# A two-layer cross-attention kernel: projections and energies of a pair moved one iteration up, beside the scores of the pair two ahead of it

## The chip, the cores and the metric

The kernel runs on one core of a Trainium2 chip. The metric is the device time of one execution in microseconds (us); less is better.

## The reference

The input is a batch of 32 items. All arithmetic is float32. Layer 0 mixes x (128 x 512 an item) with a context y of the same shape, layer 1 is an attention with 32 query heads over 8 key heads and a layer norm:

```python
def layer0(x, y, w_qk, w_v, b_v, w_t, b_t):          # x, y: (32, 128, 512)
    x_q = einsum('oc,bcn->bno', w_qk, y)
    x_k = einsum('oc,bcn->bon', w_qk, x)
    x_v = einsum('oc,bcn->bon', w_v, x) + b_v
    attention = softmax(einsum('bnc,bcm->bnm', x_q, x_k), axis=-1)
    attention = attention / (1e-07 + attention.sum(axis=1, keepdims=True))
    x_r = einsum('bcn,bnm->bcm', x_v, attention)
    return x + relu(einsum('oc,bcn->bon', w_t, x - x_r) + b_t)

def layer1(h, enc, mask, ...):                       # 32 heads of 16, 8 key heads, groups of 4
    q, k, v = h @ Wq + bq, enc @ Wk + bk, enc @ Wv + bv
    attn = softmax(q k^T / 4 + mask)                 # by head
    x = (attn v) @ Wo + bo + h
    return layernorm(x) * gamma + beta

return layer1(layer0(x, ctx, ...), ctx, mask, ...)
```

## The kernel before

The batch is worked in 16 pairs of items, j = 0 and 1. Each float32 product is made of reduced-precision parts: an operand is split in a high part, rounded by a copy into type fp32r, and a low part, the difference; a product is then high x high, high x low and low x high, three matmuls. So `xh`, `xl` are the parts of x, `yh`, `yl` of the context, `zh`, `zl` of z = (w_qk^T w_qk) x, and so on.

A pair passes through four stages, and an iteration i of the program works on several pairs at once:

- stage 0: `z_project(i)` computes z of pair i + 1.
- stage 1, pair i: `energy` (8 a pair, en00 to en13, three matmuls of 512 columns each), whose negated row maxima VectorE takes (`energy_max`) and whose exponentials ScalarE writes to `att` (`exp_energy`); `tva_project` (8 a pair: values, transposed x and more, in one), copied by ScalarE (`tva_raw`) and biased and scaled on GpSimd (`add_bias`, `scale_values`); `attend`, which sums values by attention; `layer0_out` on VectorE, which ends layer 0 and writes `x2`; `ctx_transpose` and `kv_project` for the keys and values of layer 1; `spread_k` on GpSimd.
- stage 2, pair q = i - 1: `q_project` (4 groups g), its parts `q_high` on ScalarE and `q_low` on VectorE; `max_scores`, four matmul blocks that compute all scores once for their maxima alone, and 16 `score_max` on VectorE; `max_split` makes `mrow` of them, `max_spread` turns it on TensorE, `max_rows` copies it to `mrep`; SyncE copies `qh`, `ql` into `qstack` with 12 DMAs (`stack_q`, which waits for `ql_done` of the last group) and `mrep` with one more (`stack_maxima`). Only then can `scores` run (16 blocks), ScalarE takes their exponentials (`exp_scores`), `values` sums them, `keep_sums` copies the sums to `sides`, two DMAs gather the denominators (`gather_denominators`), VectorE inverts them (`inverse_denominators`, `weigh_out`), and `at_high`, `at_low` split the result for `out_project` (wo0 in the same iteration, wo1 in the next).
- stage 3, pair i - 2: wo1, the residual add and statistics, variance and inverse root on GpSimd in small steps, `normalise`, `scale_shift`, `store`.

Each engine runs its own instructions in the written order of its function `iteration` (also `first_iteration` and `last_iteration`); semaphores connect them. Iterations 3 to 14 are a hardware loop; the rest are written out. PSUM has eight banks, handed out in a ring in the order of `WIDE_USES` (line 80): a use takes the next bank and, by `wait_slot`, waits until the use eight before it in the list has been read (`RELEASE`, line 288; for a maxima block that is its `score_max`, for a z the `z_low`). A line of this table:

```python
    ("mx01", 2), ("mx02", 2), ("mx03", 2), ("q1", 2), ("q2", 2), ("mx10", 2), ("mx11", 2), ("mx12", 2),
```

The tiles `xh`, `yh` are made on GpSimd as a product with ones (`split_x`, `split_y`, line 514), followed there by the low parts. On SyncE, the loads of the next x and y stand at `next_x`, `next_y`; `next_y(i)` waits for `ctx_transpose(i, 1)`, since the transposes read the same tile. A second copy of TensorE's program with mask matmuls (L853, L877) is taken only if the mask isn't zero; it is zero here.

## Time and profile before

| | |
|---|---|
| median of 3 runs | 855.9 us (855.87 to 859.55) |
| the profiled execution, its own time | 855.26 us |
| its span in the profile | 853.4 us |
| TensorE matmuls, busy | 763.5 us (89%) |
| VectorE | 612.0 us (72%) |
| GpSimd | 567.1 us (66%) |
| ScalarE | 481.4 us (56%) |
| mean granted TensorE clock | 0.965 |
| DMA moved | 84.88 MB |

PE is TensorE, DVE is VectorE, ACT is ScalarE, POOL is GpSimd, SP is SyncE (SPq its DMA queue). The span runs from the first to the last recorded instruction. A row in order of time gives start and length in us, and in brackets how long the engine stood idle ahead of it and which instruction released it. Matmuls overlap, so the distance of their starts and not their length is what one costs.

### The profile page before, as it was taken

Reading aid. Unit: us, or ns where it says so; the run is one execution under the profiler, and the core shown is the slowest. Engines: PE = TensorE matmul, PEld = TensorE weight load, DVE = VectorE, ACT = ScalarE, POOL = GpSimd, SP = SyncE. Lnnn points to the kernel's source line nnn. Section 1 sums busy time; section 2 is a strip of 40 time slices with the busy share of each in tenths; the row PEclk is TensorE's granted clock in tenths of the full one; section 3 lists DMA queues with packets and bytes.
Section 4 is the critical chain, followed back from the end, with each engine's and each line's share of the span. In section 5 each row is a group of like instructions: output and inputs, shape, how many; then the busy total and the mean of one; then the engine's idle time right before and its main releaser. Section 6 shows DMA issues by size and latency. Waiting matters only on the chain.

```text
span 853.4 us, 17328 instructions
## 1 busy us (share of the span) xinstructions
PE 763.5 (89%) x5015; PEld 603.7 (71%) x5015; DVE 612.0 (72%) x1016; ACT 481.4 (56%) x1067; POOL 567.1 (66%) x770
## 2 busy tenths in 40 slices
PE   5878989989898999989899999989899998988672
PEld 4766877858687786868687786868778686866531
DVE  4675876948687695958679595868869585976733
ACT  4637475564746557384756747474665738474250
POOL 4945677585766859486785948577694958664513
PEclk9889999999999999999999999999999999999776
DMA  8124242323434242343424233343413234332410
GB/s 312 67 65 114 84 112 77 99 78 111 108 97 127 74 108 74 104 120 109 103 86 118 81 93 102 111 101 98 132 68 104 77 111 114 93 77 89 95 62 25
DMA packets 55756, 84.88 MB, mean 99 GB/s; under 512 B 9520, under 2 KB 29616, under 8 KB 55600
## 3 DMA queue, kind: packets, MB, share of 16 engines
q1 hardware_dynamic: 55008, 84.25, 34.0%
q10 hardware_dynamic: 720, 0.27, 0.2%
q8 instruction: 15, 0.25, 0.1%
q14 instruction: 13, 0.11, 0.0%
HBM read 24.72 MB, written 8.39 MB: 39 GB/s over the span
## 4 chain that ended last, share of the span: by engine, by line
PE 65%; SPq 13%; DMA 7%; DVE 6%; issue 4%; POOL 3%; ACT 2%; DVEq 0%; POOLq 0%; ACTq 0%
PE banks L784 13%; SPq L374 13%; PE banks L875 8%; PE banks L888 7%; DMA qstack<-mrep 5%; PE banks L900 4%; PE banks L902 4%; PE banks L901 4%; PE banks L822 3%; DVE maxima L1522 3%; PE banks L824 3%; PE banks L823 3%; PE banks L803 2%; PE banks L846 2%; DVE ql L1515 2%
## 5 line engine op out<-in xcount | busy, mean ns | idle before, releaser
L1522 DVE TENSOR_REDUCE maxima<-banks 128x4 f32<-128x512 f32 x256 | 161.2, 688 | 8.2 <-PE banks L846 8.2
L1183 ACT ACTIVATE prob<-banks 128x512 f32<-128x512 f32 x256 | 133.4, 634 | 11.4 <-PE banks L875 11.4
L1547 DVE RECIPROCAL dens<-dens 128x512 f32<-128x512 f32 x32 | 107.3, 3353 | 39.5 <-DMA dens<-sides 39.5
L784 PE MATMUL banks<-ta,att 128*128 128x130 f32 x1024 | 119.8, 275 | 2.7 <-POOL ta L556 2.7
L784 PEld LDWEIGHTS banks<-ta,att 128*128 128x128 f32 x1024 | 118.1, 190 | 4.8 <-POOL ta L556 3.4
L1117 ACT ACTIVATE att<-banks,negmax 128x512 f32<-128x512 f32 x128 | 87.7, 688 | 51.7 <-DVE negmax L1472 51.7
L1472 DVE TENSOR_REDUCE negmax<-banks 128x1 f32<-128x512 f32 x128 | 86.6, 688 | 31.9 <-PE banks L771 30.6
L875 PE MATMUL banks<-qstack,kstack 128*128 128x512 f32 x256 | 77.8, 429 | 27.8 <-DMA qstack<-mrep 26.6
L621 POOL TENSOR_TENSOR atl<-at,ath 128x512 fp32r<-128x512 f32 x32 | 43.7, 1364 | 72.6 <-ACT ath L1195 72.1
L875 PEld LDWEIGHTS banks<-qstack,kstack 128*128 128x128 f32 x256 | 48.7, 200 | 57.9 <-issue 34.0
L549 POOL TENSOR_TENSOR ta<-ta,cb_s 128x516 f32<-128x516 f32 x64 | 76.8, 1210 | 17.1 <-ACT ta L1125 17.1
L1466 DVE TENSOR_TENSOR zl<-banks,zh 128x512 fp32r<-128x512 f32 x32 | 21.9, 685 | 77.1 <-ACT zh L1110 77.1
L822 PE MATMUL banks<-x2h,wq_h 128*128 128x256 f32 x256 | 75.3, 294 | 0.0
L824 PE MATMUL banks<-x2h,wq_l 128*128 128x256 f32 x256 | 72.2, 282 | 0.0
L823 PE MATMUL banks<-x2l,wq_h 128*128 128x256 f32 x256 | 72.1, 281 | 0.0
L1189 ACT ACTIVATE sides<-banks 128x512 f32<-128x512 f32 x64 | 39.4, 617 | 56.2 <-PE banks L888 53.3
L1195 ACT ACTIVATE ath<-at 128x512 fp32r<-128x512 f32 x32 | 20.1, 628 | 90.0 <-PE banks L902 83.4
L888 PE MATMUL banks<-prob,v 128*32 128x512 f32 x512 | 66.9, 616 | 1.2 <-ACT prob L1183 1.2
L1168 ACT ACTIVATE qh<-banks,bq_s 128x256 fp32r<-128x256 f32 x64 | 30.4, 475 | 64.5 <-PE banks L824 64.5
L1125 ACT ACTIVATE ta<-banks 128x386 f32<-128x386 f32 x128 | 60.4, 490 | 10.6 <-PE banks L759 10.6
L900 PE MATMUL banks<-wo_h,ath 128*128 128x512 f32 x128 | 54.9, 429 | 9.1 <-POOL atl L621 9.1
L561 POOL TENSOR_TENSOR late<-late,bo_b 128x512 f32<-128x512 f32 x32 | 41.1, 1286 | 30.9 <-ACT late L1174 30.9
(145 smaller groups left out, 2011.2 us busy)
## 6 DMA issues: line engine op xcount, KB each, us to landing
qstack<-qh SPq DMA_DIRECT2D x128, 128.0 KB, 2.3
xs<-in_x SPq DMA_DIRECT2D x16, 512.0 KB, 3.6
ys<-in_ctx SPq DMA_DIRECT2D x16, 512.0 KB, 3.5
kstack<-kph SPq DMA_DIRECT2D x128, 64.0 KB, 2.0
qstack<-ql SPq DMA_DIRECT2D x64, 128.0 KB, 2.3
dens<-sides SPq DMA_DIRECT2D x64, 128.0 KB, 2.0
out_x<-late SPq DMA_DIRECT2D x32, 256.0 KB, 2.1
kstack<-kpl SPq DMA_DIRECT2D x64, 64.0 KB, 2.0
```

What stands on the lines that cost most here:

```text
L374: sp.dma_start(qstack[32 * part:32 * part + 32, p].bitcast(F32), src[32 * p:32 * p + 32].bitcast(F32)).then_inc(qstack_in[p], 16)
L784: last = mm(o, att[:, j, n, bass.ts(m, P)], ta[:, j, n, 0:BW], start=n == 0, stop=n == KC - 1)
L822: mm(o, wq_h[:, k, g], x2h[:, k], start=k == 0, stop=False)
L823: mm(o, wq_h[:, k, g], x2l[:, k], start=False, stop=False)
L824: last = mm(o, wq_l[:, k, g], x2h[:, k], start=False, stop=k == KC - 1)
L875: last = mm(o, kstack[:, j, 2 * p + odd], qstack[:, p, j], start=True, stop=not masked)
L888: last = mm(banks[32 * p:32 * p + 32, slot(plan, name)], v2[:, j, 2 * p + odd], prob[:, 2 * p + odd], start=True, stop=True, tile_position ...
L900: mm(o, ath[:, g], wo_h[:, g], start=g == 0, stop=False)
L1117: nc.scalar.activation(att[:, j, n], banks[:, slot(plan, f"en{j}{n}")], exp_f, bias=negmax[:, j, n:n + 1], accum_out=rowsum[:, j, n:n + 1] ...
L1183: nc.scalar.activation(prob[:, 2 * p + odd], banks[:, slot(plan, f"st{j}{kv}")], exp_f).then_inc(sem["prob_done"], 1)
L1522: nc.vector.tensor_reduce(maxima[:, 0, :, p, :, g].rearrange("x o j -> x j o"), banks[:, slot(plan, f"mx{g}{p}")].rearrange("x (j o s) -> ...
L1547: nc.vector.reciprocal(dens[:], dens[:]).then_inc(sem["dinv_done"], 1)
```

## The change

The numbers of the two projections' stage change from 1 to 0: `tva_project`, `energy`, and what follows them (`tva_raw`, `exp_energy`, `energy_max`, `row_inverse`, `add_bias`, `scale_values`) now run in iteration i for pair i + 1, while `attend`, `layer0_out`, `ctx_transpose`, `kv_project` stay at pair i. A first iteration numbered -1 runs them for pair 0, and iteration 15 has none. `xh` and `yh` are now written by ScalarE (`x_high`, `y_high`), `at_low` is moved from GpSimd to VectorE, both `x2_low` stand in their own pair's iteration, and every engine's order and the ring's order are rewritten. The core of the diff (the other lines are of the same kind: calls in another order):

```diff
 WIDE_USES = (
-    ("en00", 1), ("en01", 1), ("en02", 1), ("wo1", 3), ("q0", 2), ("tva00", 1), ("en03", 1), ("mx00", 2),
...
+    ("q0", 2), ("q1", 2), ("q2", 2), ("mx00", 2), ("mx01", 2), ("mx02", 2), ("mx03", 2), ("wo1", 3),
+    ("mx10", 2), ("mx11", 2), ("mx12", 2), ("mx13", 2), ("q3", 2), ("et0", 1), ("et1", 1), ("mx20", 2),
+    ("mx21", 2), ("mx22", 2), ("mx23", 2), ("mx30", 2), ("mx31", 2), ("mx32", 2), ("mx33", 2), ("z0", 0),
+    ("b00", 1), ("b01", 1), ("r0", 2), ("r1", 2), ("tva00", 0), ("m", 2), ("k", 1), ("tva01", 0), ("en00", 0),
...
-                RELEASE[f"tva{j}{k}"] = ("ta_raw", 4 * j + k, 1)
-                RELEASE[f"en{j}{k}"] = ("exp_done", 4 * j + k, 1)
+                RELEASE[f"tva{j}{k}"] = ("ta_raw", 4 * j + k, 0)
+                RELEASE[f"en{j}{k}"] = ("exp_done", 4 * j + k, 0)
...
             def split_x(i, j):
-                if j == 0:
-                    pool.wait_ge(x_in, i * 16 + 16)
+                wait(pool, "xh_done", i, j)
                 wait(pool, "tva_ps", i - 1, 4 * j + 3)
-                nc.gpsimd.tensor_tensor(xh[:, j], xs[:, j], one_col, ALU.mult).then_inc(sem["xh_done"], 1)
-                wait(pool, "xh_done", i, j)
                 nc.gpsimd.tensor_tensor(xl[:, j], xs[:, j], xh[:, j].bitcast(F32), ALU.subtract
...
             def x2_low(i, j):
                 wait(pool, "x2h_done", i, j)
+                wait(pool, "k_ps", i, 0)
                 wait(pool, "v_ps", i, 0)
...
-            def energy(i, plan, j, n):
+            def energy(pair, plan, i, j, n):
                 name = f"en{j}{n}"
                 if n == 0:
-                    wait(pe, "zl_done", i, j)
-                    wait(pe, "y_split", i, j)
-                wait_slot(pe, plan, name, i)
+                    wait(pe, "zl_done", pair, j)
+                    wait(pe, "y_split", pair, j)
+                wait_slot(pe, plan, name, i, have=("zl_done", 1, j))
...
+            def x_high(i, j):
+                if j == 0:
+                    act.wait_ge(x_in, i * 16 + 16)
+                wait(act, "tva_ps", i - 1, 4 * j + 3)
+                nc.scalar.activation(xh[:, j], xs[:, j], copy_f).then_inc(sem["xh_done"], 1)
...
+            def at_low(q, j):
+                wait(dve, "ath_done", q, j)
+                wait(dve, "wo_ps", q, j - 1)
+                tt(atl[:], at[:].rearrange("p (g l) -> p g l", g=G), ath[:].bitcast(F32), ALU.subtract
+                   ).then_inc(sem["atl_done"], 1)
...
             def first_iteration(i, load_next, s1, s2, s3, setup=False):
                 if load_next:
                     next_x(i)
                 if s1:
                     next_mask(i)
-                if setup:
-                    load_late_weights()
                 if load_next:
                     next_y(i)
                 if setup:
+                    load_late_weights()
                     gather_flags()
```

In `last_iteration` (16) wo1 stands behind the maxima, both `residual_transpose` at the end behind wo0, and `values` for both odd and even heads of half 0 directly behind its eight scores.

**TensorE between the last maxima blocks and the scores, iteration 2.** L846 (now L820) is a maxima block, L757 to L759 (L731 to L733) a `tva_project`, L793 a context transpose, L832 (L806) both residual transposes, L861 (L835) `max_spread`, L769 to L771 an energy, L718 to L720 a z, L758 both `attend` of j = 0. Before:

```order
L793 MATMUL banks<-cst,ys 128x128 x4
L757 MATMUL banks<-cw_h,xh 128x386
L758 MATMUL banks<-cw_h,xl 128x386
L759 MATMUL banks<-cw_l,xh 128x258
L793 MATMUL banks<-cst,ys 128x128 x4
L832 MATMUL banks<-cst,x 128x128 x8
L861 MATMUL banks<-ident_r,mrow 128x128
L769 MATMUL banks<-zh,yh 128x512
L770 MATMUL banks<-zl,yh 128x512
L771 MATMUL banks<-zh,yl 128x512
```

and now, from the last maxima block on:

```order
L820 MATMUL banks<-kph,qh 128x256 x8
L827 MATMUL banks<-mk,cst 128x256 x8
L718 MATMUL banks<-xh,gram_h 128x512
L719 MATMUL banks<-xl,gram_h 128x512
L720 MATMUL banks<-xh,gram_l 128x512
L758 MATMUL banks<-ta,att 128x130 x16
L806 MATMUL banks<-cst,x 128x128 x8
L731 MATMUL banks<-cw_h,xh 128x386
L732 MATMUL banks<-cw_h,xl 128x386
L733 MATMUL banks<-cw_l,xh 128x258
L835 MATMUL banks<-ident_r,mrow 128x128
```

Ahead of `max_spread` now stand z and `attend` of j = 0; behind it, ahead of the scores, came three energies and now come the k projection, two `tva_project` and one energy.

**VectorE from the start of iteration 2 to the last maxima.** L1515 (L1519) is `q_low`, L1522 (L1526) `score_max`, L1472 `energy_max`, L1558 (L1568) the residual add, L1562 `at_low`, L1507 a context low part. Before:

```order
L1472 TENSOR_REDUCE negmax<-banks 128x1 x2
L1558 TENSOR_TENSOR late<-banks,late 128x512
L1472 TENSOR_REDUCE negmax<-banks 128x1
L1563 BN_STATS bns<-late 128x6
L1515 SCALAR_TENSOR_TENSOR ql<-banks,bq_s,qh 128x2x128
L1472 TENSOR_REDUCE negmax<-banks 128x1
L1522 TENSOR_REDUCE maxima<-banks 128x2x2 x2
L1568 TENSOR_SCALAR yi<-nv 128x2
L1522 TENSOR_REDUCE maxima<-banks 128x2x2
L1515 SCALAR_TENSOR_TENSOR ql<-banks,bq_s,qh 128x2x128
L1522 TENSOR_REDUCE maxima<-banks 128x2x2 x3
L1515 SCALAR_TENSOR_TENSOR ql<-banks,bq_s,qh 128x2x128
```

and now:

```order
L1562 TENSOR_TENSOR atl<-at,ath 128x512
L1519 SCALAR_TENSOR_TENSOR ql<-banks,bq_s,qh 128x2x128 x3
L1526 TENSOR_REDUCE maxima<-banks 128x2x2 x4
L1568 TENSOR_TENSOR late<-banks,late 128x512
L1526 TENSOR_REDUCE maxima<-banks 128x2x2 x2
L1573 BN_STATS bns<-late 128x6
L1526 TENSOR_REDUCE maxima<-banks 128x2x2
L1519 SCALAR_TENSOR_TENSOR ql<-banks,bq_s,qh 128x2x128
L1526 TENSOR_REDUCE maxima<-banks 128x2x2
L1507 TENSOR_TENSOR x2l<-banks,x2h 128x4x128 x2
L1526 TENSOR_REDUCE maxima<-banks 128x2x2 x3
```

Three `q_low` stand ahead of the first maximum, and the energy maxima between them are gone; the two context low parts stand in front of the third block, and `at_low` at the iteration's end.

**SyncE at the start of the program.** Before, from the second load of x on:

```order
L351 DMA xs<-in_x 128x2x512
L357 DMA mk<-in_mask 128x2x128
L405 DMA late<-in_Wq 128x4x512
L407 DMA bo_b<-in_bo 128x512
L407 DMA gamma_b<-in_gamma 128x512
L407 DMA beta_b<-in_beta 128x512
L409 DMA prob<-in_Wo 128x4x512
L354 DMA ys<-in_ctx 128x2x512
L414 DMA flag_row<-flag_col 1x128x2
```

and now:

```order
L351 DMA xs<-in_x 128x2x512
L357 DMA mk<-in_mask 128x2x128
L354 DMA ys<-in_ctx 128x2x512
L405 DMA late<-in_Wq 128x4x512
L407 DMA bo_b<-in_bo 128x512
L407 DMA gamma_b<-in_gamma 128x512
L407 DMA beta_b<-in_beta 128x512
L409 DMA prob<-in_Wo 128x4x512
L414 DMA flag_row<-flag_col 1x128x2
```

The load of the next y (`ys`), which waits for the context transposes of pair 0, stood behind the late weights and stands ahead of them.

## Rows read from the trace of the kernel before

**Rows 1.** Busy time by window: start:end, length, per engine, granted clock, DMA share, GB/s.
```profile
73.40:225.90 152.50, 143.46 (x939) 113.55 (x939) 111.15 (x186) 88.40 (x197) 102.53 (x143) 0.97 0.33 94
225.90:714.90 489.00, 464.29 (x3130) 369.38 (x3130) 371.92 (x620) 293.55 (x661) 352.45 (x481) 1.00 0.35 100
763.30:811.00 47.70, 36.77 (x254) 28.71 (x254) 29.23 (x51) 19.07 (x40) 23.44 (x39) 0.89 0.30 82
811.00:853.40 42.40, 20.41 (x72) 10.71 (x72) 13.90 (x12) 12.19 (x23) 11.53 (x28) 0.70 0.12 44
```

**Rows 2.** TensorE in order of time, one iteration: start, length, line, operation [idle before].
```profile
401.15 0.28 PE L822 MATMUL banks<-x2h,wq_h 128*128 128x256 f32 x1
...
402.58 0.34 PE L757 MATMUL banks<-cw_h,xh 128*128 128x386 f32 x1
...
411.82 0.44 PE L757 MATMUL banks<-cw_h,xh 128*128 128x386 f32 x1 [0.34 <-DVE maxima L1522]
...
417.52 0.32 PE L861 MATMUL banks<-ident_r,mrow 128*128 128x128 f32 x1 [0.32 <-DVE mrow L1537]
...
421.68 2.33 PE L875 MATMUL banks<-qstack,kstack 128*128 128x512 f32 x9 [1.52 <-DMA qstack<-mrep]
...
447.14 0.50 PE L900 MATMUL banks<-wo_h,ath 128*128 128x512 f32 x1
...
450.05 0.28 PE L822 MATMUL banks<-x2h,wq_h 128*128 128x256 f32 x1
```

**Rows 3.** The chain of waits in the same iteration: start, length, what.
```profile
411.29 0.57 SPq L374
...
418.91 2.55 DMA qstack<-mrep
```

**Rows 4.** TensorE in order of time, the first scores of iterations 1 and 2.
```profile
73.40 3.78 PE L875 MATMUL banks<-qstack,kstack 128*128 128x512 f32 x9 [1.88 <-DMA qstack<-mrep]
...
123.58 2.90 PE L875 MATMUL banks<-qstack,kstack 128*128 128x512 f32 x9 [1.99 <-DMA qstack<-mrep]
```

**Rows 5.** VectorE in order of time, the iteration of rows 2.
```profile
403.48 0.48 DVE L1515 SCALAR_TENSOR_TENSOR ql<-banks,bq_s,qh 128x256 fp32r<-128x256 f32 x1 [0.25 <-ACT qh L1168]
...
411.08 5.47 DVE L1522 TENSOR_REDUCE maxima<-banks 128x4 f32<-128x512 f32 x9
...
417.10 0.29 DVE L1537 TENSOR_REDUCE mrow<-maxima 128x64 fp32r<-128x128 f32 x1
```

**Rows 6.** TensorE in order of time, the start of the program.
```profile
20.17 0.69 PE L757 MATMUL banks<-cw_h,xh 128*128 128x386 f32 x1 [2.90 <-ACT att L1117]
...
33.28 3.84 PE L784 MATMUL banks<-ta,att 128*128 128x130 f32 x32 [1.51 <-POOL ta L556]
...
47.30 0.77 PE L769 MATMUL banks<-zh,yh 128*128 128x512 f32 x1 [2.75 <-issue]
50.03 0.59 PE L770 MATMUL banks<-zl,yh 128*128 128x512 f32 x1 [1.96 <-issue]
```

**Rows 7.** Single lines (ns min/median/max), and one group (busy us, mean ns).
```profile
L1553 DVE TENSOR_TENSOR at<-sides,dens x32: 691/693/1017, 87.8 to 832.9; 128x512 f32<-128x512 f32 x32
...
L1163 ACT ACTIVATE x2h<-x x32: 619/630/634, 45.5 to 789.5; 128x512 fp32r<-128x512 f32 x32
...
L621 POOL TENSOR_TENSOR atl<-at,ath 128x512 fp32r<-128x512 f32 x32 | 43.7, 1364 | 72.6 <-ACT ath L1195 72.1
```

**Rows 8.** SyncE in order of time, the start.
```profile
9.73 0.47 SPq L405 DMA_DIRECT2D late<-in_Wq  x1
```

**Rows 9.** TensorE in order of time, iterations 15 and 16.
```profile
763.33 2.32 PE L875 MATMUL banks<-qstack,kstack 128*128 128x512 f32 x9 [1.71 <-DMA qstack<-mrep]
...
807.51 0.47 PE L861 MATMUL banks<-ident_r,mrow 128*128 128x128 f32 x1 [4.82 <-DVE mrow L1537]
...
811.05 4.16 PE L875 MATMUL banks<-qstack,kstack 128*128 128x512 f32 x10 [1.34 <-DMA qstack<-mrep]
...
836.45 0.50 PE L900 MATMUL banks<-wo_h,ath 128*128 128x512 f32 x1 [2.12 <-POOL atl L621]
```

670 lines of the change are left out of this document (340 added, 330 removed), and 31 rows, old and new, of tables (FIRST_WIDE_USES, LAST_WIDE_USES, WIDE_USES).

## The prediction

> **What bounds the kernel now.** I read the windows by stage first. From 225.9 to 714.9 us ten iterations take 489.0 us, 48.9 each, and TensorE is busy for 464.3 of them; VectorE, the next, for 371.9 [rows 1]. So the reader is to see a matmul-bound loop with some 2.5 us an iteration in which TensorE stands still. The second view, TensorE's timeline, says where most of it lies: 0.34 us on a maxima bank, 0.32 on `mrow`, and 1.52 on the DMA of the maxima, ahead of the scores [rows 2]. Work is then 46.4 us. The third view is the chain of waits: SyncE issues the twelve stack DMAs behind `ql_done` from 411.29, comes to the DMA of `mrep` at 418.91, 7.6 later, and that DMA takes 2.55 us until the scores may go [rows 3]. Early on the same wait was longer, 1.88 and 1.99 us, and the score matmuls behind it were slow: 9 in 3.78 and 2.90 us, where 2.33 is usual [rows 4, 2]. The granted clock of that stretch is 0.97 against 1.00 later [rows 1]. Last, the two ends: iteration 16 holds only one pair's attention, and from 763.3 to 853.4 TensorE is busy for 57 us of 90 [rows 1].
>
> The sum is made against this execution: span 853.4, own time 855.26, so 1.86 lie around the span; own time is 0.6 below the median of 855.9.
>
> **Inside an iteration.** I walk the new order by rows of the old one. Time 0 is the first matmul of `q_project(0)`. A projection takes 402.58 - 401.15 = 1.43, the out-projection 450.05 - 447.14 = 2.91 [rows 2]. VectorE gives `ql` 2.33 after its projection began (403.48 - 401.15), a maximum every 0.605 (5.47 over 9), and from the last of them to `mrow` done pass 0.8 [rows 5].
> - VectorE's order now has `ql` 0, 1, 2 ahead of the first maximum. `ql` 2 starts at 2 x 1.43 + 2.33 = 5.2, so the maxima start at 5.6. Behind stand 16 maxima (9.7), `ql` 3 (0.4), the residual add, the statistics and two context subtractions (0.6 each) and the guess (0.1): 18.2; `mrow` is done at 19.0.
> - TensorE reaches the third block of maxima at about 10.8 (four projections, two blocks of maxima, out-projection, context transposes). But the ring of eight banks gives it one bank per reduced maximum: `mx33` needs `etl` 1, at 13.35, and `z0`, next in the ring, needs the maximum of `mx20`, at 13.96. It starts at 14.05. TensorE had 1.1 us of work there, some 2.2 to 2.5 idle. **The wait on the maxima DMA is so replaced by a wait on banks.**
> - From 14.05: z 0.8, attend 3.6 to 3.8 [rows 6], residual transposes 0.95, one projection 0.57: `max_spread` at 20.0, not held by `mrow` (19.0). `mrep` is copied by 20.6, its DMA takes 2.55 [rows 3], the scores may go at 23.4. TensorE meanwhile has k, two projections and an energy, 3.5 us, and comes to the scores at 23.8. That wait is gone, the stack DMAs too (11.5 + 7.6 = 19.1, ahead of `mrep`).
> - The rest is 46.4 less the 21.4 done, 25.0: end at 48.8 to 49.0. I followed the banks there: `kl` is ready 0.3 before `st04` asks, score banks come free 0.5 apart, `en03` needs the values' bias at 40.6 and comes at 41.8. None costs over 0.3; I count 0.1.
> - Idle 2.45 is what it was (2.5), so +0.1 with those. The idle now ends in blocks over 1.88 us, where the early rows show the clock fall [rows 4]. A fall over score matmuls cost 1.45 and 0.57. Here it falls on z and on attend, whose 32 loads-and-matmuls took 3.84 at a mixed clock [rows 6] against 3.7: I take half of 0.7, +0.3. **Period 49.3**, bounds 47.2 (no bank wait counts) and 50.5 (each wait drops the clock at full price).
>
> **Engines beside it.** ScalarE gets four copies of 128x512 an iteration, 0.63 each [rows 7]; it is busy 29.4 us of 48.9 [rows 1] and they stand where it waited for projections, so zero; without that cover, 2.5 us an iteration. GpSimd loses 60 products and 32 `at_low`. `x_split` still comes behind the variance on GpSimd at 13.8 and just meets `z0`; were it late, it adds one for one. `at_low` goes to VectorE, two an iteration; the nearest row there with two SBUF inputs, `at`, has 0.69 on the median and 1.02 at most, I take 0.8; GpSimd took 1.36 [rows 7]. VectorE ends its iteration at 52.4, that is 3.4 into the next, and `ql` 2 is due at 5.2: 1 us to spare after `ql` 0 and 1. Zero. On SyncE, x and y are loaded ahead of `stack_q`; x lands before 9, first used at 11.6; y is issued at 10.9 and SyncE is free again before `ql_done` at 11.5.
>
> Some `at` took 1.02 where most took 0.69, so something did hold them [rows 7]. The Trainium skill, SBUF — State Buffer, section Who interferes with whom, says of the pair of ports that VectorE and GpSimd share that a VectorE operation with two SBUF inputs and a GpSimd operation lock each other out for the whole instruction. By that rule an `at_low` that meets a GpSimd operation waits for all of it, and the move costs what rival 3 works out from rows, 854 in place of 846.
>
> **Head.** Before, the scores of iteration 1 began at 73.40 [rows 4]. Now pair 0's projections and energies are in iteration -1 (no mask sums on ScalarE ahead of them) and end at about 22.5, against the 2.9 us wait of before; attends run 23.4 to 30.8, where they stood from 33.28 on [rows 6]. Pair 1's z, 8 projections and 8 energies, 11 us, come into iteration 0, paced by VectorE (two `layer0_out`, the selectors, `wq_l`, energy maxima): end at 47.5, an estimate of mine and the weakest number here. The flag's load and jump then cost the 2.75 + 1.96 of before [rows 6]. First `q_project` at 52, scores 23.8 later: 76. **+2.6**. SyncE: `load_late_weights` was issued at 9.73 [rows 8]; now `next_y(0)` is ahead of it and waits for pair 0's context transposes, at 23.4; the weights then land by 33, before `wq_l` needs them at 44. Bounds: 72 to 80.
>
> **Iteration 15 and the end.** Iteration 15 now has no projections, z or energies: 11.3 us less on TensorE. It is then bound by VectorE and the denominators: maxima chain as above, scores at 22.4, last `at_low` at 46.0. Iteration 16's maxima need 12.1 more of VectorE, `mrow` at 58.1, scores at 61.7, 39.3 after those of 15. Before it was 811.05 - 763.33 = 47.7, with 4.82 lost on `mrow` [rows 9]. **-8.4**; bounds -5 and -10. From there to the end 42.4 [rows 1]: both o-values of half 0 come earlier by about 1, and an `at_low` of 0.7 to 0.8 in place of 1.36 is in the chain twice (2.12 of wait ahead of the last out-projection [rows 9]). **-2.1**; bounds 0 and -3.
>
> **Sum.** Scores 1 to scores 15 took 763.33 - 73.40 = 689.9 [rows 9, 4]. Now 14 x 49.3 less 1.4, since iteration 15 comes to its scores earlier: 688.8, **-1.1** (the early slow scores go, the steady ones cost a little). 853.4 + 2.6 - 1.1 - 8.4 - 2.1 = 844.4; with 1.86 around it **846**. With the terms' bounds together, its own range is 838 to 854.
>
> **Rivals.**
> 1. *Slower: the bank wait drops the clock in each iteration.* Place: TensorE ahead of `z_project(0)`. Full price 1.45 [rows 4, 2] instead of 0.3: 14 x 1.15 = 16, so 862. It decides where the walked idle of 2.2 to 2.5 is real: 1.52 left the clock up [rows 2], 1.88 and 1.99 did not [rows 4]. Against: small matmuls lie in it, and attend is bound by weight loads. The Trainium skill, TensorE: Matmul & The Clock Gate, section HAM oscillation, says that a wait that comes back each tile can start the array slow each time; the early rows agree, the steady 1.52 do not. Chance 0.17.
> 2. *No wait at all.* If banks come free earlier than I walked (VectorE starts its maxima sooner), 2.1 of the idle goes: 14 x 2.1 = 29, so 817. For: VectorE is idle 11.7 us an iteration [rows 1]. Against: the ring ties TensorE to it just here. Chance 0.12.
> 3. *The order is better but VectorE is not.* Each `at_low` held by a GpSimd operation, 0.69 + 1.36 = 2.0 instead of 0.8 [rows 7]: 2.4 more an iteration, 1 of it covered; with half of them met, some 0.6 x 14 = 8, so 854. Or the late weights hold iteration 1 by 5: 851. Or it does not do what it says, the two ends' gains failing: 855. Chance 0.13.
>
> **Chances.** A measurement of this kernel can tell 0.5%, 4.3 us: faster is below 851.6, slower above 860.2. Forecast 0.58, of it 0.05 above 851.6. Faster 0.53 + 0.12, same 0.05 + 0.13, slower 0.17, rounded to 0.66, 0.18, 0.16. The range takes in the forecast's own, most of rival 3, and reaches into rivals 1 and 2, leaving 0.2 out: 830 to 860.
>
> **What will show it.** Idle ahead of the scores near zero and some 2 us ahead of `gram_h` z matmuls, put down to maxima; scores 49.3 apart; scores 1 near 76; scores 15 to 16 near 39. It is wrong if idle of over 1 us stands at the scores again, if `ql` waits for VectorE's end of the iteration before, or if the clock of the steady stretch is below 0.97.

## The result, and the profile after

The changed kernel took 865.25 us (median of 4 runs, 863.56 to 865.70), the kernel before beside it 857.02 (4 runs, 855.87 to 859.55): a ratio of 1.009, with an interval of 1.006 to 1.012. It is 0.9% **slower**, where I had forecast 846. The profiled execution took 863.56, its span is 861.8.

The first lines of the page, busy time by engine:

```profile
PE 777.9 (90%) x5015; PEld 623.9 (72%) x5015; DVE 623.3 (72%) x1048; ACT 504.4 (59%) x1128; POOL 473.8 (55%) x677
```

ScalarE and VectorE have more to do than before, GpSimd 93 us less, as the diff says. TensorE has the same 5015 matmuls and is busy 14 us longer: the same work runs slower. Windows of the profile after, columns as in [rows 1]:

```profile
229.43:730.54 501.11, 477.37 (x3131) 384.07 (x3131) 376.31 (x641) 309.17 (x701) 294.21 (x420) 0.98 0.34 98
355.10:404.04 48.94, 46.58 (x314) 37.30 (x313) 37.61 (x65) 30.84 (x71) 29.42 (x42) 1.00 0.35 100
404.04:454.62 50.58, 48.20 (x315) 38.81 (x313) 37.66 (x65) 30.96 (x71) 29.38 (x42) 0.97 0.33 97
778.53:821.23 42.70, 33.11 (x199) 24.00 (x200) 27.64 (x41) 15.27 (x33) 13.51 (x17) 0.86 0.33 92
821.23:861.80 40.57, 20.10 (x80) 11.78 (x80) 15.94 (x15) 14.67 (x27) 18.59 (x46) 0.71 0.12 46
```

The first line holds the same ten iterations as the second of [rows 1] (scores 4 to scores 14): 501.1 us instead of 489.0. The second and third are two neighbouring iterations, 7 and 8: 48.94 us at clock 1.00, and 50.58 at 0.97. By stage, with the forecast beside it:

| stretch (starts on TensorE) | before | forecast | after |
|---|---|---|---|
| start to scores 1 | 73.4 | 76 | 81.6 |
| scores 1 to 15 | 689.9 | 688.8 | 697.0 |
| scores 15 to 16 | 47.7 | 39.3 | 42.7 |
| scores 16 to the end | 42.4 | 40.3 | 40.6 |

**Inside iteration 8.** TensorE in order of time, columns as in [rows 2]; L796 is the first query projection, L820 a maxima block, L874 wo1, L718 z, L758 attend, L849 the scores:

```profile
404.04 0.28 PE L796 MATMUL banks<-x2h,wq_h 128*128 128x256 f32 x1
...
409.70 0.71 PE L820 MATMUL banks<-kph,qh 32*128 32x256 f32 x8 [1.18 <-DVE ql L1519]
410.34 0.50 PE L874 MATMUL banks<-wo_h,ath 128*128 128x512 f32 x1
...
417.57 0.38 PE L820 MATMUL banks<-kph,qh 32*128 32x256 f32 x2 [0.49 <-DVE maxima L1526]
418.17 0.38 PE L820 MATMUL banks<-kph,qh 32*128 32x256 f32 x1 [0.21 <-DVE x2l L1507]
418.76 0.50 PE L820 MATMUL banks<-kph,qh 32*128 32x256 f32 x5 [0.22 <-DVE x2l L1507]
419.54 0.50 PE L718 MATMUL banks<-xh,gram_h 128*128 128x512 f32 x1 [0.27 <-POOL xl L508]
...
420.57 5.14 PE L758 MATMUL banks<-ta,att 128*128 128x130 f32 x32
...
430.20 1.38 PE L849 MATMUL banks<-qstack,kstack 128*128 128x512 f32 x5
431.42 3.73 PE L758 MATMUL banks<-ta,att 128*128 128x130 f32 x32
```

The 1.5 us ahead of the scores [rows 2] are gone, as forecast. What stands still is 1.18 us ahead of the first maxima block, which waits for `ql`, and 0.49, 0.21, 0.22 and 0.27 around the last two blocks and z. The sum is 2.37 us; it was 2.46 before, and I had walked 2.2 to 2.5. But attend of j = 0 takes 5.14 us (420.57) where the same 32 loads and matmuls of j = 1 take 3.73 (431.42). In iteration 7, by the starts of the rows, z takes 0.79 us, attend 3.57 and the residual transposes 0.79; in iteration 8 they take 1.03, 4.98 and 0.79. The clock by windows, the sparse stretch and what follows, in iteration 7 (first two lines) and 8:

```profile
367.10:371.10 4.00, 2.80 (x21) 1.67 (x20) 4.00 (x8) 1.49 (x3) 2.90 (x10) 1.00 0.62 181
371.10:374.10 3.00, 3.00 (x27) 2.92 (x26) 3.00 (x7) 1.64 (x3) 1.77 (x9) 1.00 0.93 205
416.04:420.04 4.00, 2.80 (x21) 1.68 (x20) 4.00 (x8) 1.51 (x3) 2.89 (x10) 1.00 0.55 179
420.04:423.04 3.00, 3.00 (x14) 2.83 (x14) 3.00 (x7) 1.63 (x3) 1.76 (x9) 0.50 0.97 220
```

In iteration 7 the granted clock stays at 1.00 (2.4 GHz) after TensorE was busy 2.8 of 4 us; in iteration 8, after the same 2.80 of 4, it is 0.50 (1.2 GHz). Each wait of iterations 4 to 14 agrees to 0.03 us with the same wait of the others, and yet nine of the iterations 1 to 14 take 50.5 to 50.6 us (1, 3, 5, 6, 8, 9, 11, 12, 14) and, from 4 on, the others 48.94 to 48.97. **An iteration without a fall is as long as before (48.9); a fall costs 1.64 us.** Nine of them are 14.8 us, on a kernel that is 8 slower.

**VectorE, the same place** (L1551 inverts denominators, L1568 is a residual add, L1562 `at_low`, L1519 `ql`, L1526 maxima), and under it GpSimd (L534 `add_bias`, L508 the low part of x):

```profile
402.08 3.34 DVE L1551 RECIPROCAL dens<-dens 128x512 f32<-128x512 f32 x1
...
406.21 0.68 DVE L1568 TENSOR_TENSOR late<-banks,late 128x512 f32<-128x512 f32 x1
...
407.54 1.63 DVE L1562 TENSOR_TENSOR atl<-at,ath 128x512 fp32r<-128x512 f32 x1
409.10 1.25 DVE L1519 SCALAR_TENSOR_TENSOR ql<-banks,bq_s,qh 128x256 fp32r<-128x256 f32 x3
410.44 2.49 DVE L1526 TENSOR_REDUCE maxima<-banks 128x4 f32<-128x512 f32 x4
```

```profile
407.42 1.20 POOL L534 TENSOR_TENSOR ta<-ta,cb_s 128x516 f32<-128x516 f32 x1 [3.60 <-ACT ta L1110]
...
418.14 1.27 POOL L508 TENSOR_TENSOR xl<-xs,xh 128x512 fp32r<-128x512 f32 x1
```

`ql` starts 5.06 us after the projection (409.10 - 404.04), behind VectorE's work for the iteration before, which ended at 5.1 and not at 3.4. `at_low` there takes 1.63 us, with GpSimd operations from 407.42 beside it. Over all 32 the median is 1.02, and I had taken 0.8. The price is paid on both sides: the `add_bias` that starts while an earlier `at_low` runs (399.77) takes 1.65 us, where the one at 407.42 takes 1.20.

**Head and end.** The start on VectorE (L1442 copies the selectors, L1490 begins `layer0_out`), the two copies as single operations, what GpSimd does beside them, and TensorE; then TensorE and one row of VectorE in iterations 15 and 16, and the clock of the last out-projection of iteration 15:

```profile
33.01 5.77 DVE L1442 CAST kstack<-cst 32x1024 fp32r<-32x1024 f32 x2
38.79 0.16 DVE L1490 TENSOR_SCALAR colneg<-banks 128x4 f32<-128x4 f32 x1
```

```profile
L1442 DVE CAST kstack<-cst x2: 677/2922/5166, 33.0 to 38.1; 32x1024 fp32r<-32x1024 f32 x2
```

```profile
34.10 3.53 POOL L502 MEMSET qstack<- 128x4096 f32 x1
```

```profile
39.96 0.55 PE L777 MATMUL banks<-x2h,wkv_h 128*128 128x256 f32 x1 [4.20 <-DVE ta L1496]
...
55.50 0.55 PE L796 MATMUL banks<-x2h,wq_h 128*128 128x256 f32 x1 [3.70 <-issue]
```

```profile
778.53 1.39 PE L849 MATMUL banks<-qstack,kstack 128*128 128x512 f32 x5 [1.62 <-DMA qstack<-mrep]
...
796.93 0.79 PE L874 MATMUL banks<-wo_h,ath 128*128 128x512 f32 x1 [3.77 <-DVE atl L1562]
...
821.23 3.75 PE L849 MATMUL banks<-qstack,kstack 128*128 128x512 f32 x8 [3.07 <-DMA qstack<-mrep]
```

```profile
805.85 0.48 DVE L1519 SCALAR_TENSOR_TENSOR ql<-banks,bq_s,qh 128x256 fp32r<-128x256 f32 x1 [0.96 <-ACT qh L1154]
```

```profile
796.93:802.22 5.29, 5.29 (x13) 4.13 (x14) 3.95 (x2) 0.72 (x5) 2.32 (x2) 0.50 0.34 108
```

The v projection waits 4.20 us for a bank that `layer0_out` of j = 1 frees, and that stands behind 5.77 us of selector copies. The first copy takes 5.17 us and the second, with nothing on GpSimd beside it, 0.68; GpSimd is at the low part of y until 34.17 and clears `qstack` until 37.63, and the first copy ends 0.55 behind that. In the kernel before, the two took 1.69 and 1.54. So most of the 5.77 looks like the same sharing as in `at_low`; no run moved GpSimd's part alone. In iteration 15 wo0 waits 3.77 us for `at_low`, and its twelve matmuls then take 5.29 us at 0.50 in place of 2.91 [rows 2]. From scores 15 on the mean clock is 0.86, and in the last stretch 0.71 (the last two windows above).

### The profile page after: what moved, and what is told of

It is laid out like the page before. It is cut to its first block, busy times and chain, and to the rows that moved or that the text cites. A ratio compares the mean times of both kernels' runs of the same rounds, so it can differ in the third digit from the quotient of the medians.

```text
span 861.8 us, 17461 instructions
## 1 busy us (share of the span) xinstructions
PE 777.9 (90%) x5015; PEld 623.9 (72%) x5015; DVE 623.3 (72%) x1048; ACT 504.4 (59%) x1128; POOL 473.8 (55%) x677
## 4 chain that ended last, share of the span: by engine, by line
PE 61%; DVE 18%; issue 10%; POOL 5%; DMA 2%; ACT 1%; DVEq 1%; POOLq 1%; ACTq 0%; SPq 0%
PE banks L758 14%; PE banks L849 8%; PE banks L862 7%; DVE dens L1551 6%; DVE maxima L1526 3%; PE banks L745 3%; PE banks L744 3%; PE banks L743 3%; PE banks L874 2%; PE banks L731 2%; PE banks L732 2%; PE banks L876 2%; PE banks L875 2%; POOL xl L508 2%; PE banks L777 2%
## 5 line engine op out<-in xcount | busy, mean ns | idle before, releaser
L1169 ACT ACTIVATE prob<-banks 128x512 f32<-128x512 f32 x256 | 138.5, 609 | 44.4 <-PE banks L849 44.3
L1526 DVE TENSOR_REDUCE maxima<-banks 128x4 f32<-128x512 f32 x256 | 160.6, 683 | 1.2 <-PE banks L820 0.2
L758 PEld LDWEIGHTS banks<-ta,att 128*128 128x128 f32 x1024 | 133.5, 210 | 2.9 <-issue 0.4
L758 PE MATMUL banks<-ta,att 128*128 128x130 f32 x1024 | 133.4, 294 | 0.2 <-DVE maxima L1526 0.2
L1551 DVE RECIPROCAL dens<-dens 128x512 f32<-128x512 f32 x32 | 107.1, 3346 | 17.8 <-DMA dens<-sides 17.8
L534 POOL TENSOR_TENSOR ta<-ta,cb_s 128x516 f32<-128x516 f32 x64 | 83.2, 1301 | 50.1 <-ACT ta L1110 50.1
L602 POOL TENSOR_TENSOR x2l<-x,x2h 128x512 fp32r<-128x512 f32 x32 | 41.5, 1299 | 93.0 <-ACT x2h L1149 93.0
L849 PE MATMUL banks<-qstack,kstack 128*128 128x512 f32 x256 | 81.1, 430 | 4.7 <-DMA qstack<-mrep 4.7
L849 PEld LDWEIGHTS banks<-qstack,kstack 128*128 128x128 f32 x256 | 44.6, 192 | 52.8 <-ACT prob L1169 38.6
L820 PE MATMUL banks<-kph,qh 32*128 32x256 f32 x512 | 52.3, 349 | 32.1 <-DVE ql L1519 17.3
L796 PE MATMUL banks<-x2h,wq_h 128*128 128x256 f32 x256 | 75.3, 294 | 3.8 <-issue 3.7
L820 PEld LDWEIGHTS banks<-kph,qh 32*128 32x128 f32 x512 | 30.9, 182 | 54.9 <-issue 24.0
L874 PE MATMUL banks<-wo_h,ath 128*128 128x512 f32 x128 | 56.5, 441 | 9.0 <-DVE atl L1562 8.8
L796 PEld LDWEIGHTS banks<-x2h,wq_h 128*128 128x128 f32 x256 | 49.6, 194 | 7.0 <-issue 3.9
```

The costliest lines, as they stand in the source:

```text
L534: nc.gpsimd.tensor_tensor(part, part, cb_s[:].unsqueeze(1).broadcast_to([P, 2, X0]), ALU.add).then_inc(sem["ta_done"], 1)
L758: last = mm(o, att[:, j, n, bass.ts(m, P)], ta[:, j, n, 0:BW], start=n == 0, stop=n == KC - 1)
L796: mm(o, wq_h[:, k, g], x2h[:, k], start=k == 0, stop=False)
L820: last = mm(banks[:, slot(plan, name), 2 * P * j:2 * P * (j + 1)], qh[rows, j, g], kph[rows, j], start=True, stop=not masked)
L849: last = mm(o, kstack[:, j, 2 * p + odd], qstack[:, p, j], start=True, stop=not masked)
L874: mm(o, ath[:, g], wo_h[:, g], start=g == 0, stop=False)
```

## Experiments

Each kernel was timed beside the kernel before on the same chip; the chip differs between groups of runs, so "ratio", which is to the kernel before, is what compares them. "Falls" are those of iterations 1 to 14 that are over 1 us (in e7 0.7) longer than the quiet ones, with attend (in e7 the scores) at the low clock. They are counted in the one profiled execution, which need not be a typical one of its kernel: in e6 (845.6) and e14 (862.6) it is the longest, in e2 (856.6) and e13 (858.9) the shortest.

| run | median, us | ratio (95%) | falls | quiet iteration |
|---|---|---|---|---|
| the change | 865.2 | 1.009 (1.006 to 1.012) | 9 | 48.95 |
| e1, filler ahead of `ql` | 863.2 | 1.010 (1.006 to 1.013) | 8 | 48.8 |
| e2, selectors late | 859.4 | 1.004 (1.002 to 1.006) | 8 | 48.9 |
| e3, VectorE's end moved | 864.8 | 1.010 (1.007 to 1.014) | 9 | 48.95 |
| e4, `at_low` on GpSimd | 844.3 | 0.987 (0.980 to 0.995) | 6 | 47.9 |
| e5, 8 fillers at the blocks | 865.0 | 1.011 (1.006 to 1.016) | 0 | 50.03 |
| e6, e4 and e2 | 839.4 | 0.979 (0.974 to 0.984) | 7 | 47.9 |
| e7, e6 and wo1 moved | 881.5 | 1.032 (1.027 to 1.036) | 9, at the scores | 50.7 |
| e8, e6 and 8 fillers | 849.8 | 0.993 (0.990 to 0.995) | 0 | 48.97 |
| e9, e6 and 4 fillers | 847.2 | 0.990 (0.988 to 0.992) | 4 | 48.3 |
| e10, 4 fillers | 867.5 | 1.016 (1.013 to 1.019) | 8 | 49.3 |
| e11, second `at_low` alone | 855.0 | 1.001 (0.999 to 1.004) | 6 | 48.55 |
| e12, high parts on GpSimd | 884.2 | 1.033 (1.029 to 1.037) | all | none |
| e13, e6, transposes moved | 871.8 | 1.021 (1.013 to 1.029) | 8 | 48.3 |
| e14, before with `at_low` on VectorE | 859.5 | 1.004 (1.002 to 1.006) | none of this kind | 49.05 |

### What makes the clock fall: e1, e5, e8

e1 fills the largest wait, ahead of `ql`, with matmuls that change nothing:

```diff
+                if g == 0:
+                    wait_slot(pe, plan, "mx00", i)
+                    for _ in range(5):
+                        mm(banks[:, slot(plan, "mx00")], gram_h[:], wq_h[:, 0].rearrange("p g c -> p (g c)"),
+                           start=True, stop=True)
                 wait(pe, "ql_done", q, g)
```

> The changed kernel with five redundant matmuls of 512 columns (128x128 weights, result overwritten) on TensorE ahead of its wait for ql, in the bank that the first maxima block owns already. They add 1.1 us of TensorE work an iteration inside the 1.18 us in which it stood still, and leave every other wait as it is. In the changed kernel 8 of 12 steady iterations take 50.6 and 4 take 48.95 with the same waits to 0.02 us; the slow ones have z and attend of j = 0 at a lower clock. Theory A (the waits are free in themselves, it is the clock that falls after them, 1.65 us each): adding work makes the kernel faster, all iterations near 48.95 to 49.1, total 850 to 853, mean clock of the steady stretch 1.00. Theory B (TensorE is simply held by VectorE and the clock is a by-product of load elsewhere): no change, 864 to 867, or the added 1.1 us shows where the filler overruns the wait.

Measured: 863.2, eight falls. Theory A fell in this form: the wait ahead of `ql` is gone, the idle time of an iteration is halved (1.19 us left of 2.37), and the clock falls nearly as often. So the place matters, and e5 fills the other one, 8 to 10 us later:

```diff
                             wait_slot(pe, plan, name, i, have=("ql_done", -1, g))
+                            if (g, p) in ((2, 0), (3, 0), (3, 2), (3, 3)):
+                                for _ in range(2):
+                                    mm(banks[:, slot(plan, name)], gram_h[:], wq_h[:, 0].rearrange("p g c -> p (g c)"),
+                                       start=True, stop=True)
```

> The changed kernel with eight redundant matmuls of 512 columns an iteration (1.8 us of work, each in a bank that the following maxima matmul owns and overwrites) spread over the third and fourth maxima blocks, where TensorE waits bank by bank for VectorE and is busy 0.42, 0.66 and 0.73 in the three microseconds before its granted clock is 0.50. The run with filler ahead of ql, 7 us earlier, left 8 of 14 iterations at 50.3 to 50.6. Theory A (it is the sparse stretch just ahead of z that drops the clock): no iteration near 50.6, all 48.9 to 49.3, total 849 to 854. Theory B (the clock does not fall for sparseness of this stretch): 863 to 868, iterations at 50.6 as before, or longer by filler that does not fit.

Measured: 865.0, and no fall in 14 iterations. Theory A holds for the clock; my time for it was wrong, since eight fillers are too long for the stretch, z comes 1.1 us later, and each iteration takes 50.03. The median is that of the change by coincidence: 1.1 us of filler in 14 iterations for nine falls of 1.64. e8 puts the same filler into e6, the best version, which has both e4's and e2's edits (shown below):

> The kernel with at_low on GpSimd and late selectors, plus the eight redundant matmuls in the third and fourth maxima blocks. Theory A (sparseness there drops the clock): the 5 to 6 iterations at 49.2 to 49.6 become 47.9 to 48.1 as well, 6 to 9 us below the run without filler, 829 to 834. Theory B: as the run without filler, or up to 2 us an iteration slower where filler does not fit.

Again none of 14 falls, again z is 1.1 us late (48.97 for 47.9). The time, 849.8, is 10 us above e6, where I had expected it 6 to 9 below. The clock of the same 487 us in e8 (first) and e6 (second), and the sparse stretch of e8 on TensorE with the fillers (L833):

```profile
227.00:714.00 487.00, 480.60 (x3192) 378.10 (x3192) 354.48 (x619) 307.65 (x695) 307.50 (x439) 1.00 0.34 101
```

```profile
227.00:714.00 487.00, 472.14 (x3125) 378.54 (x3124) 354.99 (x620) 310.04 (x700) 309.23 (x440) 0.98 0.34 101
```

```profile
407.83 0.72 PE L833 MATMUL banks<-wq_h,gram_h 128*128 128x512 f32 x2 [0.32 <-DVE maxima L1542]
408.48 0.38 PE L836 MATMUL banks<-kph,qh 32*128 32x256 f32 x2
408.79 0.74 PE L833 MATMUL banks<-wq_h,gram_h 128*128 128x512 f32 x2
409.46 0.38 PE L836 MATMUL banks<-kph,qh 32*128 32x256 f32 x1
...
410.86 0.50 PE L730 MATMUL banks<-xh,gram_h 128*128 128x512 f32 x1
```

The attend matmuls show it over a whole execution (busy, mean ns of one), for before, e5 and the change:

```profile
L784 PE MATMUL banks<-ta,att 128*128 128x130 f32 x1024 | 119.8, 275 | 2.7 <-POOL ta L556 2.7
```

```profile
L758 PE MATMUL banks<-ta,att 128*128 128x130 f32 x1024 | 119.6, 275 | 0.0
```

```profile
L758 PE MATMUL banks<-ta,att 128*128 128x130 f32 x1024 | 133.4, 294 | 0.2 <-DVE maxima L1526 0.2
```

Before and with all gaps filled: 275 ns. In the change: 294 ns, 13.6 us over 1024 of them. That is where most of TensorE's 14 us went.

### Half the filler, and needed work instead: e9, e10, e13, e7

e9 is e8, and e10 is e5, with one matmul in place of the two:

```diff
-                                for _ in range(2):
-                                    mm(banks[:, slot(plan, name)], ...
+                                mm(banks[:, slot(plan, name)], ...
```

> The kernel with at_low on GpSimd and late selectors, with one redundant matmul at each of the four places in the third and fourth maxima blocks where there were two before (0.9 us of filler an iteration instead of 1.8). With eight of them no iteration had z and attend at the low clock, but z came 1.1 us later than without (steady 48.97 against 47.9 or 49.2 to 49.55). Theory A (sparseness there drops the clock, and half the filler is enough and fits): all iterations 47.9 to 48.2, total 829 to 835. Theory B (only a stretch without any idle keeps the clock): falls come back in about half the iterations, 836 to 842.

> The changed kernel as it stands with the same four redundant matmuls an iteration. With eight of them all its iterations took 50.03, none at the low clock, z 1.1 us later. Theory A: four fit without delay, all iterations 48.95 to 49.2, total 849 to 853, and the step from 865 is the price of the falls alone. Theory B: falls stay, 860 to 866.

One filler in each place left four and eight falls, and z was still 0.4 us late: theory B in both, though 847.2 and 867.5 lie above its 836 to 842 and 860 to 866, which leave that delay out. The stretch from the third block to z is idle for 1.2 us without filler, for 0.5 with four and for 0.3 with eight. Only the nearly full stretch kept the clock in each iteration, and filler that full costs two thirds of a fall, each time. e13 moved the two context transposes, 1.0 us, between the third and the fourth block:

```diff
+                if s2:
+                    max_scores(q, plan, i, 2, masked)
                 if s1:
                     ctx_transpose(i, plan, 0)
                     ctx_transpose(i, plan, 1)
                 if s2:
-                    max_scores(q, plan, i, 2, masked)
                     max_scores(q, plan, i, 3, masked)
```

> The kernel with at_low on GpSimd and late selectors (839.4), with the eight context transposes (1.0 us on TensorE) between the third and fourth maxima blocks instead of ahead of the third, and the two context low parts moved with them on VectorE. No work is added. Theory A (needed work in the sparse stretch does what the redundant one did): z as early as before, 14.4 after the first q_project, falls in fewer than 4 of 14 iterations, 832 to 838. Rival (transposes count as sparse too, or the k projection now waits for the later context parts): 839 to 846.

871.8, outside both forecasts. The four executions took 858.9, 867.3, 876.2 and 878.8, the widest spread of all, and even the first lies above every one of e6. That first one is the one profiled: eight falls, and from iteration 10 on longer ones, 51.0 to 51.2. The clock now falls already inside the fourth block, in iteration 11 some 0.6 us ahead of 557.5, as the 0.91 of the first line says:

```profile
554.00:557.50 3.50, 2.34 (x16) 1.18 (x13) 3.50 (x7) 1.71 (x3) 2.68 (x10) 0.91 0.29 108
557.50:564.00 6.50, 6.20 (x27) 5.92 (x28) 5.72 (x12) 2.97 (x5) 5.15 (x16) 0.52 0.90 234
```

This does not test which kind of matmul keeps the clock. The transposes were only moved, and what they filled opened again elsewhere: an iteration is idle for 1.8 to 1.9 us where e6 is idle for 1.5, 0.6 to 0.7 of it ahead of z, behind the low part of x. Whether transposes added as filler would do what matmuls of 512 columns did stays open. e7 used wo1, 2.9 us of full matmuls, with its VectorE and GpSimd work moved behind it:

```diff
-                if s3:
-                    out_project(i - 2, plan, i, 1)
                 if s2:
                     max_scores(q, plan, i, 1, masked)
...
                     max_scores(q, plan, i, 2, masked)
+                if s3:
+                    out_project(i - 2, plan, i, 1)
...
-                if s3:
-                    variance(i - 2)
                 if split_next:
                     split_x(i + 1, 0)
                 if s3:
+                    variance(i - 2)
                     newton_root(i - 2)
```

> The kernel with at_low on GpSimd and late selectors, with wo1 (2.9 us of dense matmuls that are needed anyway) moved from behind the first to behind the third maxima block; its residual add and statistics on VectorE and the variance on GpSimd move with it, behind the low part of x. Theory A (real work in the sparse stretch): z starts near 13.4 in place of 14.4, no clock fall ahead of it, iterations 46.9 to 47.6, total 820 to 830. Against: mrow and its DMA come no earlier, so the wait moves back to the scores (0.5 to 1.5 us there): 47.9, total 832 to 838, or the clock falls elsewhere.

881.5, outside both forecasts. At its new place wo1 does what theory A says: no attend of j = 0 in iterations 1 to 14 is at the low clock. But the statistics come later too, GpSimd's variance and root with them, and in my order the low part of y stands behind the root. An energy waits for it, and the clock falls there, over the scores:

```profile
431.63 0.72 PE L754 MATMUL banks<-zh,yh 128*128 128x512 f32 x1 [2.23 <-POOL yl L514]
```

### What makes VectorE late: e3, e4, e11, e14

e3 only reorders VectorE: what closed an iteration now stands between the first steps of the next.

```diff
                     weigh_out(q, 1)
-                    residual_add(q, plan, 0)
...
-                    row_statistics(q, 0)
-                    at_low(q, 1)
...
                     q_low(q, plan, 0)
+                    residual_add(i - 2, plan, 0, behind=True)
                     q_low(q, plan, 1)
+                    at_low(i - 2, 1)
                     q_low(q, plan, 2)
                     score_max(q, plan, 0, 0)
                     score_max(q, plan, 0, 1)
+                    row_statistics(i - 2, 0)
```

> The changed kernel with three VectorE operations moved over the loop's end: the residual add of wo0 stands behind ql 0, the second at_low behind ql 1, the statistics behind the second maximum. Nothing is added or left out. Theory A (VectorE comes 1.2 us late to ql, and that backlog makes the waits that drop the clock): the 1.18 us wait ahead of the first maxima block is gone, z starts near 14.2 after the first q_project in place of 15.5, iterations 47.7 to 48.3 without a clock fall, total 838 to 848. Theory B (the backlog is only moved; banks wait as long as before, the clock still falls ahead of z): 860 to 865.

864.8, nothing gained: theory B. TensorE's wait moved from `ql` (1.18) to wo1, which waits 1.12 us for `at_low`; z starts 15.5 after the projection as before. VectorE now stands idle ahead of the first `ql`, since ScalarE's `qh` is not there yet (this iteration's projection starts at 406.11):

```profile
409.90 0.48 DVE L1519 SCALAR_TENSOR_TENSOR ql<-banks,bq_s,qh 128x256 fp32r<-128x256 f32 x1 [1.47 <-ACT qh L1154]
```

The second `at_low` takes 0.93 us in its new place and not 1.63, but the idle time and the moved operations behind it use that up: the maxima start 6.43 after the projection, 6.40 in the change. This order is worth nothing. e4 takes work out, and has in GpSimd's `iteration`:

```diff
                     residual_bias(q, 1)
+                    at_low(q, 0)
...
                     add_bias(i + 1, 1, 1)
+                if s2:
+                    at_low(q, 1)
                 if s0:
                     scale_values(i + 1, 0)
```

> The changed kernel with both at_low on GpSimd again (before x2_low of j = 0, and behind the last add_bias). Takes 1.2 to 1.4 us an iteration from VectorE, half of it from the stretch ahead of ql. Theory A (VectorE's backlog decides): ql comes 0.6 to 1 us earlier, fewer iterations at 50.6, total 850 to 858. Theory B (the move to VectorE was free, the 1.28 us GpSimd operation is the slower one and the last at_low now comes later for wo1): 864 to 872.

844.3 (840.6 to 852.1), 2.1% below the change by the two ratios, and better than the 850 to 858 of theory A. The first `ql` starts 3.1 after the projection instead of 5.06 (401.55 - 398.45):

```profile
401.55 0.95 DVE L1531 SCALAR_TENSOR_TENSOR ql<-banks,bq_s,qh 128x256 fp32r<-128x256 f32 x2 [0.23 <-ACT qh L1166]
```

```profile
402.28 1.27 POOL L607 TENSOR_TENSOR atl<-at,ath 128x512 fp32r<-128x512 f32 x1
```

z comes 1.05 us earlier, quiet iterations take 47.9, and there are six falls where there were nine. e11 has only the second of the two lines, `at_low(q, 1)`; the first stays on VectorE:

> The changed kernel with only the second at_low (the one at VectorE's end of the iteration, behind the statistics) on GpSimd; the first stays on VectorE. Theory A (what costs is the backlog just ahead of ql): the whole gain of moving both, iterations 47.9 and 49.5, median 841 to 848. Rival (VectorE's sum of work decides, each at_low half): iterations 48.4 and 50.0, 852 to 857.

855.0, quiet iterations of 48.55, six falls: the rival. The first `at_low`, 948 ns on VectorE there in the mean, delays what is behind it too, though it starts 8.4 us ahead of `ql`. Is the operation itself at fault? e14 takes both from GpSimd in the kernel before:

```diff
                     layer0_out(i, plan, 0)
+                    at_low(q, 0)
                     k_low(i, plan)
...
                     layer0_out(i, plan, 1)
+                    at_low(q, 1)
```

> The kernel before, with both at_low on VectorE, each behind a layer0_out, where VectorE had idle time around it. Theory A (the operation costs only where VectorE is late for TensorE): iterations of 48.9 as before, and the end 1 to 1.4 us shorter, 853 to 856. Rival (each at_low delays VectorE's end of the iteration and so ql and the maxima, 1.2 to 1.4 us an iteration): 865 to 875.

859.5: 0.4% slower (1.002 to 1.006), near theory A but not free, and the end is not shorter. In the profiled execution, the longest of ten, steady iterations take 49.04, +0.14 each, and iterations 1, 3 and 15 take 1.9, 2.4 and 2.0 us more, the first two with 3.3 and 4.3 us of DMA wait ahead of their scores. The operation's rows in the change and in e14 (ns min/median/max; then busy, mean ns):

```profile
L1562 DVE TENSOR_TENSOR atl<-at,ath x32: 675/1022/1632, 101.3 to 844.1; 128x512 fp32r<-128x512 f32 x32
```

```profile
L1547 DVE TENSOR_TENSOR atl<-at,ath 128x512 fp32r<-128x512 f32 x32 | 21.9, 683 | 2.5 <-ACT ath L1184 2.4
```

0.68 us where GpSimd stood still, up to 1.63 where it did not. This holds one by one: all 32 of e14 and the one at 803.79 in the change have no GpSimd operation beside them and take 0.68 to 0.69; in iterations 1 to 14 of the change each of the 28 has one under way when it starts, and takes 0.93 to 1.63.

### The other parts: e2, e6, e12

e2, in VectorE's `first_iteration`:

```diff
-                    setup_selectors()
                     layer0_out(i, plan, 1)
...
                     row_inverse(i + 1, 1)
+                    setup_selectors()
```

> The changed kernel with the two selector copies on VectorE (5.77 us) behind the last row inverse of iteration 0 instead of ahead of layer0_out of j = 1. Theory A (they hold layer0_out, so the v projection waits 4.20 us for its bank and the clock then stays low from 39.96 to 44.4): the wait goes, the low stretch too, first q_project at 50 to 52 in place of 55.5, total 4 to 6 us less, 859 to 861. Rival: the weights of q (2.29 us on VectorE at 48.3) and the flag set the start of iteration 1 anyway, or the selectors now hold the first ql: 0 to 2 us less, 863 to 865.

859.4, 4 us less than the change by the ratios. The v projection no longer waits, the first `q_project` starts at 49.07 instead of 55.50, and 1.78 us come back as a wait for the first `ql`, behind the copies' new place.

> The changed kernel with both at_low on GpSimd and with the selector copies behind the row inverses, the two edits of the runs before together. If they are independent, 844.3 - 5.9 = 838.4 with first q_project near 50 and iterations of 47.9 or 49.5: 835 to 841. If the later selectors now hold the first maxima of iteration 1, only half of it: 841 to 844.

839.4: the two edits add up. **This version is 2.1% faster than the kernel before** (0.974 to 0.984) and 2.9% faster than the change. Its longest execution, the one profiled, still has seven falls in it.

e12 undoes the move of the high parts (the same for y, and ScalarE's `x_high`, `y_high` of the next pair go):

```diff
-                wait(pool, "xh_done", i, j)
                 wait(pool, "tva_ps", i - 1, 4 * j + 3)
+                nc.gpsimd.tensor_tensor(xh[:, j], xs[:, j], one[:].broadcast_to([P, N]), ALU.mult).then_inc(sem["xh_done"], 1)
+                wait(pool, "xh_done", i, j)
```

> The changed kernel with the high parts of x and y (from the second pair on) made on GpSimd again, each ahead of its low part. Theory A (x_split only just met z: it came 0.27 us late, behind the variance): the extra GpSimd operation of 1.3 us goes one for one into the wait ahead of z, 14 x 1.3 = 18 us, and a longer sparse stretch lets the clock fall in all iterations rather than 9 of 14, 7 more: 880 to 892. Rival (free, as ScalarE's copies were costed at nothing, GpSimd having room): 863 to 867.

884.2, theory A. GpSimd ends the low part of x at 429.1, z has waited 1.37 us in place of 0.27, and in none of iterations 1 to 14 does the clock hold:

```profile
429.20 0.79 PE L725 MATMUL banks<-xh,gram_h 128*128 128x512 f32 x1 [1.37 <-DVE maxima L1520]
```

So ScalarE's copies are worth 19 us to this order of work (2.4% by the ratios). I had costed them at nothing as a load on ScalarE, which was right, and not seen that the rest leans on them.

## Why the prediction was wrong

The forecast was 846 us, faster; it came out at 865.2, outside the range. The loop failed by the mechanism of rival 1, which had a chance of 0.17 and said 862. That this number lies near is partly luck: rival 1 put 16 us of falls on the loop, which missed by 8.2, and the other 9 of the 17.4 us come from the head and iteration 15, which it left as they were.

Of the three signs of being wrong, one came: `ql` waits for VectorE's end of the iteration before. No idle of over 1 us stood at the scores of the loop, and its clock was 0.98, above the 0.97 that I had set.

- **The walk of an iteration was right in its sum, and in part by luck.** It gave 48.8 to 49.0 without a clock fall; quiet iterations take 48.94 to 48.97. The wait at the scores is gone, as it said. But it had put all of its 2.2 to 2.5 us of idle on banks ahead of z. Only 1.19 stand there, 0.27 of them for the low part of x on GpSimd; the other 1.18 are a late VectorE, which the walk had in time. In e4, where it is in time, a quiet iteration is idle for 1.5 and takes 47.9. So the walk was 1 us too long, and VectorE's lateness hid it.
- **"I take half of 0.7, +0.3" was the step that failed.** I reasoned that attend is bound by weight loads and barely slows; its 5.14 against 3.73 us shows that it does. With the end of z (four of the nine times) it makes up the whole of a fall, 1.64; the transposes behind it do not slow. In 9 of 14 iterations that is +1.05 an iteration instead of +0.3. The rows I had to go by said it (1.45 over scores [rows 4]); I discounted them with a reason that no row showed. e5 and e8 show that the sparse stretch at the last two blocks is the cause, since filled it never falls. The filler also delays z by 1.1 us, but delay alone does not help: in e12 z starts as late as in e5, 16.6 us after the projection, without filler, and the clock falls in all 14.
- **"VectorE ends its iteration at 52.4, that is 3.4 into the next ... 1 us to spare" was wrong**: it ends at 5.1. The two `at_low` took 0.95 and 1.63 and not 0.8 each, which is 1.0 of the 1.7; the rest lies in the walk of VectorE before them. In the walk this was hidden, because maxima were to start at 5.6 anyhow; TensorE's first block came at 5.66 and VectorE's maxima at 6.4, and z at 15.5 for 14.05. e4 prices `at_low` on VectorE as a whole, held or not: 2.1%, 18 us. Rival 3 named the mechanism (an `at_low` held by a GpSimd operation, up to 2.0 us) and priced it at 8 us; what the hold alone costs, without the 0.68 of the operation itself, no run shows. The Trainium skill, SBUF — State Buffer, section Who interferes with whom, has VectorE and GpSimd lock each other out over their shared ports. The trace agrees: up to 1.63 with GpSimd at work and 0.68 without, and 1.65 for 1.20 on GpSimd's side.
- **Head, +2.6, measured +8.2.** I called its 47.5 the weakest number. TensorE's work for iteration 0 ended at 51.8, since the selector copies (5.77 us) hold `layer0_out`. I had listed them and given them no length; the trace of before has 3.2 for the two, and beside GpSimd's clearing of `qstack` they took 2.6 more. e2 gives the price, 6.4 us at the first projection and 4 in the time. The rest is iteration 1's scores at 26.1 after its first projection for 23.8.
- **Iteration 15 to 16, -8.4, measured -5.0.** The last `at_low` ends 25.9 us after the scores for the 23.6 that I had walked; what took these 2.3 of the 3.4, at a mean clock of 0.86, no run separates. And I forgot that wo0 stands between `at_low` and the next projection on TensorE, and runs at the low clock after its wait, 5.29 us: the projections come late, VectorE stands 0.96 us idle for `qh`, and the maxima end 1.2 later than walked.
- **End, -2.1, measured -1.8.** Right; e4, with `at_low` on GpSimd, takes 41.7 there for the 40.6 of the change. The copies on ScalarE at nothing and the SyncE order: nothing shows against them, and no run tried the SyncE order by itself.

By stage the misses are 5.6 in the head, 8.2 in the steady part, 3.4 and 0.3 behind it: 17.5 together, against 861.8 - 844.4 = 17.4.

The Trainium skill, TensorE: Matmul & The Clock Gate, section HAM oscillation, was the rule against me: a wait that comes back each tile can start the array slow each time. The trace agrees in kind: in nine of 14 iterations attend runs slow. The section's case is one long DMA wait a tile; here several short waits do it.

## What to carry to other kernels

Price a stall twice: its own length, and what the matmuls behind it take at half clock, in whatever they are, weight-load-bound or not; use the dearest row at hand until one shows less. Several short waits among small matmuls can be worse than a single one of 1.5 us, so look at the density of the microseconds around a wait and not at its length alone. When work is moved to an engine, walk what that engine does in the stretch just ahead of the bottleneck, with durations taken beside a busy neighbour, and undo each part by itself: here one part of the change cost 2.1% and another was worth 2.4%.
